# The first router of a mixture-of-experts block: eleven of 32 slot marks made by ScalarE, one group's logits computed between the next group's transposes, gather indices taken straight from the sums, and the passing of rows moved later

## The chip, the cores and the metric

The kernel runs on one core of a Trainium2 chip. The metric is the time of one execution on the device in microseconds (us), where lower is better. TensorE is called PE here, its weight loads PEld, VectorE DVE, ScalarE ACT, GpSimd POOL and SyncE SP, as in the rows of the profile.

## The reference, cut to what matters

4096 rows of 256 numbers go through three residual blocks: half a mixture-of-experts layer, a linear-attention layer with its own feed-forward part, and half a mixture-of-experts layer again. The change is in the first of them:

```
x = x + 0.5 * ffn(layernorm(x), w_switch, b_switch, w1, b1, w2, b2)

def ffn(x, ...):                       # x: 4096 rows, 8 experts, capacity 256
    probs  = softmax(x @ w_switch + b_switch)
    routes = probs.argmax(-1);  pmax = probs.max(-1)
    oh   = routes[:, None] == arange(8)
    pos  = (cumsum(oh, axis=0) * oh).sum(-1) - 1     # place in the expert's queue
    keep = pos < 256
    slot = where(keep, routes * 256 + pos, none)
    h = relu(rows_of_slots @ w1[e] + b1[e]);  y = h @ w2[e] + b2[e]
    out = where(keep, y[slot], x) * (pmax / stop_gradient(pmax))
```

A row that found no place keeps its own value. So each expert's first 256 rows are gathered, computed, and written back, and every row is also scaled and stored as if it had not been kept; the kept ones are overwritten.

## The kernel before, in words

**The work around the change.** The 4096 rows are 32 tiles of 128 rows (`NT`), in 8 groups of 4 tiles (`NG`, `GROUP`) and two batches of 16 tiles (`BATCH`). Every engine runs its own program, written out by hand in order; semaphores join them, and an instruction that waits holds all that stand behind it on its engine. Nothing is reordered by a scheduler.

**The pass over the rows.** SP loads the groups into `x_all`. PE transposes each tile (`turn_x`) into one of three PSUM banks, ACT copies it out (`turned_rows`); DVE takes mean and variance (`stats_a`). For each group PE then computes the logits (`logits_a`, which needs ACT's copies of that group and its copy of the logits before), ACT copies them out (`logits_out`), PE transposes them back (`turn_logits`). In each iteration PE does the four transposes of group g, then the logits of group g-1, then turns those of g-2.

**The router.** For each batch, DVE finds the best expert (`choose_a`, ten operations in the first batch, eight in the second), PE counts how many rows chose it earlier (`count_a`), and DVE makes from the count each row's place and one mark per tile: a 128x256 matrix in bf16 that is 1 where the place equals the column (`marks_a`). PE multiplies marks with row numbers (`number_slots_a`), which leaves in PSUM which row stands in each of the 2048 slots. DVE reduces these sums to `number_a`, makes of them the slot numbers and `token`, the indices of the gathers, and then the factors (`weigh_a`, `split_factors_a`).

**The experts.** GpSimd gathers the rows of an expert in two halves (`load_rows`), and gives 1/sqrt(variance) (`root_half`, `root_rows`); DVE normalises (`norm_rows`), PE transposes (`turn_rows`) and does two matrix products in units u of a quarter expert (`up`, and `down` two units later). For expert x, unit j, u is 4x+j. ACT does the first halves of the weights' high/low split (`high_weights`), DVE the second (`low_weights`). GpSimd sends finished rows with `send_rows(x)` at u = 4x+5; for expert 0 it first waits until all eight groups are stored (`s_astored`).

**Passing rows.** ACT scales the rows of a group in `x_all` (`pass_rows`), and SP stores the group in `mid_rows` (`store_quad`). Groups 0 to 3 are passed before the experts, 4 and 5 behind the first two copies of turned rows, 6 and 7 in units 0 to 3. SP also issues the experts' weight loads in the same queue: in step u of its loop it loads the weights of unit u+8, and the second load of such a pair waits until `down` of unit u is done.

## Time and profile before

| | |
|---|---|
| median of 3 runs | 696.75 us (694.77 to 698.53) |
| the profiled execution | 692.72 us, its span 691.0 us |
| PE busy | 648.0 us of the span |
| DVE, ACT, GpSimd busy | 517.4, 462.8 and 367.4 us |
| bytes moved by DMA | 95.61 MB, mean 138 GB/s |

The span is what the trace covers, and the execution's own time is 1.7 us more. A timeline row has start, length, engine, line, operation and tiles, and in brackets how long the engine stood idle before it and what ended that. Times in rows count from the start of the span; the length of "x4" is that of all four together. The expert phase of the first block begins at 44.37 us.

### The profile page before, as it was taken

The numbers are of one execution on the slowest core, as the hardware profiler recorded it, in microseconds if no ns is written. First come the engines' busy times: TensorE is split into PE (matmuls) and PEld (weight loads), VectorE is DVE, ScalarE is ACT, GpSimd is POOL, SyncE is SP. The second block draws the span as 40 slices with busy tenths as digits, with TensorE's granted clock in tenths as the row PEclk, the third lists the DMA queues.
The fourth block names the chain that finished last, engine by engine and source line by source line (L and its number), as shares of the span: only waits on it lengthen the run. The fifth ranks groups of instructions, "written<-read, shape, count | busy, mean of one in ns | idle before, by whom it ended". The sixth has DMA issues, their size and how long they took to land.

```text
span 691.0 us, 18005 instructions
## 1 busy us (share of the span) xinstructions
PE 648.0 (94%) x6398; PEld 570.5 (83%) x6398; DVE 517.4 (75%) x1371; ACT 462.8 (67%) x923; POOL 367.4 (53%) x542
## 2 busy tenths in 40 slices
PE   7789999997789999999999999999999994999997
PEld 5559998975679898988888888888988783899997
DVE  7968797624678877868778778888767558799982
ACT  6687777605467786767767667776763654798882
POOL 5254454634867545464673764845635653454422
PEclk9789999999999999999999999999999996999999
DMA  8499979424765555544565565564451534577750
GB/s 262 140 295 309 289 220 333 142 80 81 112 112 98 97 95 78 116 73 76 103 90 122 80 97 122 69 115 83 64 115 26 174 101 108 176 221 240 225 166 31
DMA packets 284803, 95.61 MB, mean 138 GB/s; under 512 B 213988, under 2 KB 281664, under 8 KB 284714
## 3 DMA queue, kind: packets, MB, share of 16 engines
q1 hardware_dynamic: 267610, 82.27, 49.4%
q0 software_dynamic: 4992, 11.47, 6.0%
q10 hardware_dynamic: 12112, 0.72, 1.1%
q8 instruction: 52, 0.85, 0.5%
q14 instruction: 37, 0.30, 0.1%
HBM read 65.09 MB, written 29.40 MB: 137 GB/s over the span
## 4 chain that ended last, share of the span: by engine, by line
PE 51%; DVE 8%; POOL 5%; issue 5%; ACT 3%; SPq 3%; DMA 1%; ACTq 1%; POOLq 0%; DVEq 0%
PE bank L1990 46%; PE bank L1999 5%; SPq L453 2%; POOL hids L920 2%; DMA qkv_rows<-feats 1%; SPq L459 1%; DVE den L1810 1%; DVE kv_ L1835 1%; DVE hn_ L1855 1%; DVE att_ L1808 1%; POOL sth L905 1%; ACTq L453 1%; POOL stz L889 1%; DVE ots L1801 0%; DVE feats L1930 0%
## 5 line engine op out<-in xcount | busy, mean ns | idle before, releaser
L1990 PE MATMUL bank<-hnts,up_w 128*128 128x512 f32 (+1 forms) x432 | 106.1, 382 | 0.1
L1990 PE MATMUL bank<-down_w,hids 128*128 128x256 f32 x768 | 104.5, 284 | 1.2 <-POOL hids L920 0.4
L920 POOL TENSOR_TENSOR hids<-hid,hids 128x512 fp32r<-128x512 f32 (+1 forms) x67 | 82.0, 1225 | 36.3 <-ACT hids L1212 36.2
L1990 PEld LDWEIGHTS bank<-down_w,hids 128*128 128x128 f32 x768 | 96.6, 189 | 4.2 <-POOL hids L920 1.8
L1990 PEld LDWEIGHTS bank<-hnts,up_w 128*128 128x128 f32 x432 | 71.3, 189 | 10.3 <-ACT hids L1212 0.3
L1990 PE MATMUL bank<-qkv_w,xnts 128*128 128x256 f32 (+1 forms) x384 | 76.9, 348 | 2.9 <-DVE xnts L1821 2.4
L1990 PEld LDWEIGHTS bank<-qkv_w,xnts 128*128 128x128 f32 x384 | 60.6, 189 | 20.0 <-issue 5.8
L1207 ACT ACTIVATE hid<-bank,cols 128x512 f32<-128x512 f32 (+1 forms) x72 | 45.7, 640 | 39.8 <-PE bank L1990 39.4
L886 POOL TENSOR_SCALAR stz<-stz 128x1 f32<-128x1 f32 x32 | 7.2, 226 | 115.2 <-DVE stz L1839 115.2
L1990 PE MATMUL bank<-xa_xt,a_w 128*128 128x256 f32 x384 | 52.6, 287 | 1.6 <-ACT xa_h L1048 1.1
L1990 PE MATMUL bank<-xb_xt,b_w 128*128 128x256 f32 x384 | 50.2, 280 | 0.7 <-DVE xb_xt L1502 0.5
L1990 PEld LDWEIGHTS bank<-xa_xt,a_w 128*128 128x128 f32 x384 | 47.9, 189 | 3.2 <-issue 1.5
L1990 PE MATMUL bank<-b_w2p,xb_hs 128*128 128x256 f32 x360 | 48.7, 285 | 0.0
L1990 PEld LDWEIGHTS bank<-xb_xt,b_w 128*128 128x128 f32 x384 | 47.4, 188 | 1.4 <-DVE xb_xt L1502 1.0
L1990 PEld LDWEIGHTS bank<-b_w2p,xb_hs 128*128 128x128 f32 x360 | 45.3, 191 | 0.0
L1212 ACT ACTIVATE hids<-bank,cols 128x512 fp32r<-128x512 f32 (+1 forms) x72 | 45.2, 635 | 0.0
L811 POOL DMA_INDIRECT mid_rows<-xa_fin,xa_slot x16 | 20.1, 1256 | 37.7 <-DVE xa_fin L1570 35.6
L811 POOL DMA_INDIRECT out_dram<-xb_fin,xb_slot x16 | 18.4, 1152 | 36.5 <-DVE xb_fin L1570 27.4
L1207 ACT ACT_TABLE_LOAD x29 | 37.2, 1283 | 0.5
L1855 DVE TENSOR_SCALAR hn_<-xo,sth 128x256 f32<-128x256 f32 x32 | 25.9, 808 | 15.5 <-POOL sth L905 15.1
L1048 ACT ACTIVATE xa_h<-bank,cols 128x256 f32<-128x256 f32 x64 | 26.7, 468 | 15.0 <-PE bank L1990 15.0
L1048 ACT ACTIVATE xb_h<-bank,cols 128x256 f32<-128x256 f32 x64 | 26.8, 470 | 14.8 <-PE bank L1990 14.8
(299 smaller groups left out, 1637.7 us busy)
## 6 DMA issues: line engine op xcount, KB each, us to landing
qkv_rows<-feats SPq DMA_DIRECT2D x32, 384.0 KB, 2.7
a_raw<-in_L_ffn_w_dram SPq DMA_DIRECT2D x32, 256.0 KB, 4.6
a_w<-in_L_ffn_w_dram SPq DMA_DIRECT2D x32, 256.0 KB, 4.7
b_raw<-in_L_ffn_w_dram SPq DMA_DIRECT2D x32, 256.0 KB, 3.4
b_w<-in_L_ffn_w_dram SPq DMA_DIRECT2D x32, 256.0 KB, 3.2
mid_rows<-x_all SPq DMA_DIRECT2D x8, 512.0 KB, 4.5
values<-qkv_rows SPq DMA_DIRECT2D x32, 128.0 KB, 3.0
late_rows<-x_ SPq DMA_DIRECT2D x8, 512.0 KB, 3.1
```

The source lines that it names most:

```text
L453: engine.dma_start(keys[i][t * HEADS:(t + 1) * HEADS, :, t * HD:(t + 1) * HD], qkv_rows[1, rows, :].rearrange("(s t) (h d) -> t h s d", t= ...
L459: engine.dma_start(queries[i][t * HD:(t + 1) * HD, :, t * HEADS:(t + 1) * HEADS], qkv_rows[0, rows, :].rearrange("(s t) (d h) -> t d s h", ...
L811: pool.indirect_dma_start(ex.target, bass.IndirectOffsetOnAxis(ap=ex.buf.slot[:, c - ex.first * ST], axis=0), ex.buf.fin[c % 4][:], None, ...
L886: pool.tensor_scalar(st[:, 8:9], st[:, 7:8], EPS, None, ALU.add).then_inc(s_rsz, 1)
L889: pool.tensor_tensor(st[:, 8:10], st[:, 8:10], minus_half[:, 0:2], ALU.pow).then_inc(s_rsz, 1)
L920: pool.tensor_tensor(hids[1][u % 3][:, 0:w], hid[u % 2][:, 0:w], f32(hids[0][u % 3][:, 0:w]), ALU.subtract).then_inc(s_hidl, 1)
L1048: act.activation(ex.buf.h[u % 4][:, i], dst[:, i * CAP:(i + 1) * CAP], ACT.Relu, bias=bias).then_inc(ex.sem.relu, 1)
L1207: act.activation(hid[u % 2][:, i * w:(i + 1) * w], bank[b][:, i * w:(i + 1) * w], ACT.Gelu, bias=cols[:, C_FCB + m:C_FCB + m + 1]).then_in ...
L1212: act.activation(hids[0][u % 3][:, i * w:(i + 1) * w], bank[b][:, i * w:(i + 1) * w], ACT.Gelu, bias=cols[:, C_FCB + m:C_FCB + m + 1]).the ...
L1855: dve.tensor_scalar(hn[:], xo[n % 3][:], st[:, 6:7], st[:, 8:9], ALU.subtract, ALU.mult).then_inc(s_hn, 1)
L1990: return pe.matmul(dst, left, right, start=start, stop=stop, skip_group_check=True)
L1999: return pe.matmul(dst, src, ident[:], is_transpose=True, start=start, stop=stop, skip_group_check=True)
```

## The change

Seven things are done:

- ACT makes 8 of the first batch's 16 marks and 3 of the second's, each with two operations instead of DVE's one: the absolute value of (place - column), and then relu(1 - that). DVE makes the other 21.
- PE computes the logits of group g-1 ahead of the last transpose of group g, and counts the first batch after its loop instead of ahead of the logits of group 6. ACT's conversion of the first expert's weights is cut in two, with the marks between.
- `token` is made from `number_a` in one operation (minus 1, at least 0), before the slot numbers instead of after them.
- PE does six products whose results nobody reads (`idle_products`), each of 512 columns, while it waits for the second batch.
- `weigh_a` is cut in two: the sum and its reciprocal are `top_a`, and the last two operations stand behind the second batch's marks.
- The first batch's marks by ACT are multiplied after the second count, ahead of the second batch's.
- Three groups instead of four are passed before the experts, one behind each half of the turned rows, and the last three in units 0 to 5. SP stores groups 0 to 4 ahead of its loop, and groups 5, 6 and 7 in steps u = 1, 3 and 5 of it, behind that step's weight loads.

```diff
@@ -473,6 +473,7 @@
         chunks = [(i, k, c) for i, (_, n, parts) in enumerate(pieces) for k in range(n)
                   for c in range(0, parts[-1][1] + parts[-1][2], D)]
         LATE = 10
+        PASSED_FIRST = 3
         LN_OF = {2: 2}
...
-            return 6 * b + 2
+            return 4 * b + 2
         def weighed(b):
-            return 11 * b + 6
+            return 9 * b + 8
+
+        def topped(b):
+
+            return 11 * b + 4
         def factored(b):
             return 9 * b + 13
+
+        MARKS_BY_ACT = (8, 3)
+
+        def marked_by_act(b):
+
+            return range((b + 1) * BATCH - MARKS_BY_ACT[b], (b + 1) * BATCH)
+
+        def marked_by_dve(b):
+
+            return range(b * BATCH, (b + 1) * BATCH - MARKS_BY_ACT[b])
+
+        def act_marks(b, half):
+
+            return NT + 2 * sum(MARKS_BY_ACT[:b]) + half * MARKS_BY_ACT[b]
         number_sums = bank[7][:, 0:E * ST * 2]
...
@@ -605,7 +624,7 @@
                     sp.wait_ge(xa.sem.rows[0][ST - 1], 16)
                     for c in range(PAIRS):
                         load_weights(1, xa, c)
-                if g < NG - 1:
+                if g < PASSED_FIRST + ST:
                     store_quad(g)
@@ -623,8 +642,8 @@
                 x, j = divmod(u, PAIRS)
                 if x + 2 < E:
                     load_weights(x + 2, xa, j)
-                if u == 0:
-                    store_quad(NG - 1)
+                if u % 2 == 1 and PASSED_FIRST + ST + u // 2 < NG:
+                    store_quad(PASSED_FIRST + ST + u // 2)
                 if u == LATE - 4:
                     sp.wait_ge(s_atab, 4)
...
@@ -1055,7 +1074,7 @@
                 for s in range(ST):
                     turn_half(s, ex)
                     if ex.first == 0:
-                        pass_rows(NG // 2 + s)
+                        pass_rows(PASSED_FIRST + s)
                 for u in range(ex.first * PAIRS, ex.end * PAIRS + 2):
                     x, j = divmod(u, PAIRS)
                     if x < ex.end:
@@ -1084,6 +1103,16 @@
                 these = slice(b * BATCH, (b + 1) * BATCH)
                 act.wait_ge(s_apick, 8 * b + 4)
                 act.activation(ex_a[:, these], sub_a[:, these], ACT.Exp).then_inc(s_aexp, 1)
+
+            def marks_a(b):
+                act.wait_ge(s_adisp, placed(b))
+                for n in marked_by_act(b):
+                    act.activation(mark_a[n][:], place[:], ACT.Abs, bias=small_a[:, 2, n:n + 1],
+                                   scale=-1.0).then_inc(s_axt, 1)
+                for i, n in enumerate(marked_by_act(b)):
+                    act.wait_ge(s_axt, act_marks(b, 0) + i + 1)
+                    act.activation(mark_a[n][:], mark_a[n][:], ACT.Relu, bias=first_wins[:, 0, E - 1:E],
+                                   scale=-1.0).then_inc(s_axt, 1)
             def pass_rows(g, part=range(GROUP)):
                 for n in range(g * GROUP + part.start, g * GROUP + part.stop):
...
@@ -1104,18 +1133,22 @@
                     logits_out(g - 1)
                 if g == NG - 1:
                     soften_a(0)
-            for c in range(PAIRS):
+            for c in range(PAIRS // 2):
+                high_weights(0, xa, c)
+            marks_a(0)
+            soften_a(1)
+            marks_a(1)
+            for c in range(PAIRS // 2, PAIRS):
                 high_weights(0, xa, c)
             act.wait_ge(s_mean, 2)
             act.copy(cols[:], bank[2][:, 0:col_rows]).then_inc(s_cols, 1)
-            soften_a(1)
-            for g in range(NG // 2):
+            for g in range(PASSED_FIRST):
                 pass_rows(g)
             def middle_weights(u):
-                if u < 2 * ST:
-                    pass_rows(NG // 2 + ST + u // 2, range(u % 2 * 2, u % 2 * 2 + 2))
+                if u < 2 * (NG - PASSED_FIRST - ST):
+                    pass_rows(PASSED_FIRST + ST + u // 2, range(u % 2 * 2, u % 2 * 2 + 2))
                 if LATE <= u < LATE + chunks_through(2):
                     i, k, c = chunks[u - LATE]
...
@@ -1571,13 +1604,22 @@
                                              scalar=ex.buf.scale[:, c - ex.first * ST], in1=buf[:, s], op0=ALU.mult,
                                              op1=ALU.add).then_inc(ex.sem.fin, 1)
+            def number_slots_a():
+
+                dve.tensor_scalar(empty_a[:], number_a[:], 0.0, float(NOWHERE + 1), ALU.is_equal, ALU.mult).then_inc(s_atab, 1)
+                dve.wait_ge(s_atab, 2)
+                dve.scalar_tensor_tensor(out=slot_a, in0=number_a[:], scalar=-1.0, in1=empty_a[:], op0=ALU.add,
+                                         op1=ALU.add).then_inc(s_atab, 1)
+
             def run_experts(ex, between=None, meanwhile=None):
                 if ex.slots is None:
-                    dve.wait_ge(s_atab, 3)
-                    dve.tensor_scalar(ex.buf.token[:], ex.buf.slot[:, :, 0], T - 1, None, ALU.min).then_inc(ex.sem.token, 1)
+                    dve.wait_ge(s_atab, 1)
+                    dve.tensor_scalar(ex.buf.token[:], number_a[:], -1.0, 0.0, ALU.add, ALU.max).then_inc(ex.sem.token, 1)
+                    number_slots_a()
                     dve.wait_ge(s_bias_raw, 16 * 7)
                     dve.tensor_copy(spread[:], ln_last[:].broadcast_to([1, P])).then_inc(s_foldq, 1)
                     split_factors_a(0)
+                    top_a(1)
                     weigh_a(1)
                     split_factors_a(1)
                 first_rows(ex, meanwhile)
...
@@ -1663,17 +1705,21 @@
                     dve.wait_ge(s_aseen, 2 * b + 2)
                     dve.tensor_tensor(seen_a[:, b + 1], recent_a[:, b], seen_a[:, b], ALU.add).then_inc(s_aseen, 1)
-            def weigh_a(b):
-                these, step = slice(b * BATCH, (b + 1) * BATCH), weighed(b) - 4
-                total, top, root = (small_a[:, i, these] for i in (3, 4, 0))
+            def top_a(b):
+                these, step = slice(b * BATCH, (b + 1) * BATCH), topped(b) - 2
+                total, top = (small_a[:, i, these] for i in (3, 4))
                 dve.wait_ge(s_aexp, b + 2)
                 dve.tensor_reduce(total, ex_a[:, these], AX, ALU.add).then_inc(s_adisp, 1)
                 dve.wait_ge(s_adisp, step + 1)
                 dve.reciprocal(top, total).then_inc(s_adisp, 1)
-                dve.wait_ge(s_adisp, step + 2)
+
+            def weigh_a(b):
+                these, step = slice(b * BATCH, (b + 1) * BATCH), weighed(b) - 2
+                top, root = (small_a[:, i, these] for i in (4, 0))
+                dve.wait_ge(s_adisp, topped(b))
                 dve.reciprocal(root, top).then_inc(s_adisp, 1)
-                dve.wait_ge(s_adisp, step + 3)
+                dve.wait_ge(s_adisp, step + 1)
                 dve.scalar_tensor_tensor(out=factor_a[:, these], in0=top, scalar=0.5, in1=root, op0=ALU.mult,
                                          op1=ALU.mult).then_inc(s_adisp, 1)
...
                 dve.wait_ge(s_adisp, step + 1)
                 dve.tensor_reduce(pos, cnt_a[:, these], AX, ALU.add).then_inc(s_adisp, 1)
                 dve.wait_ge(s_adisp, step + 2)
-                for n in range(b * BATCH, (b + 1) * BATCH):
+                for n in marked_by_dve(b):
                     dve.tensor_scalar(mark_a[n][:], place[:], small_a[:, 2, n:n + 1], None,
                                       ALU.is_equal).then_inc(s_amark, 1)
...
             marks_a(0)
             choose_a(1)
+            top_a(0)
+            marks_a(1)
             weigh_a(0)
-            marks_a(1)
             slot_a, scale_a = xa.buf.slot[:, :, 0], xa.buf.scale[:, :, 0]
             dve.wait_ge(s_aslot, NT)
             dve.tensor_reduce(number_a[:], number_sums.rearrange("p (c f) -> p c f", f=2), AX, ALU.add).then_inc(s_atab, 1)
-            dve.wait_ge(s_atab, 1)
-            dve.tensor_scalar(empty_a[:], number_a[:], 0.0, float(NOWHERE + 1), ALU.is_equal, ALU.mult).then_inc(s_atab, 1)
-            dve.wait_ge(s_atab, 2)
-            dve.scalar_tensor_tensor(out=slot_a, in0=number_a[:], scalar=-1.0, in1=empty_a[:], op0=ALU.add,
-                                     op1=ALU.add).then_inc(s_atab, 1)
             def middle_weights(u):
...
                     mm(dst[:, j + 1:], ones_bf[:], hot_a[:, b0 + j:b0 + j + 1].broadcast_to([P, BATCH - 1 - j, E]))
                 mm(dst, ones_bf[:], seen_a[:, b:b + 1].broadcast_to([P, BATCH, E]), stop=True).then_inc(s_acount, 1)
-            def number_slots_a(b):
+            def number_slots_a(b, rows):
                 sums = number_sums.rearrange("p (e s f) -> p s e f", s=ST, f=2)
                 pe.wait_ge(s_apick, 8 * (b + 1))
-                for n in range(b * BATCH, (b + 1) * BATCH):
-                    pe.wait_ge(s_amark, n + 1)
+                for n in rows:
+                    if n in marked_by_dve(b):
+                        pe.wait_ge(s_amark, n + 1 - sum(MARKS_BY_ACT[:b]))
+                    else:
+                        pe.wait_ge(s_axt, act_marks(b, 1) + n + 1 - rows.start)
                     for s in range(ST):
                         last = mm(sums[:, s], mark_a[n][:, s * P:(s + 1) * P], left_number_a[:, n], n == 0 and s == 0,
                                   n == NT - 1)
                     last.then_inc(s_aslot, 1)
             pe.wait_ge(s_pool_const, 6)
-            for g in range(NG + 2):
+            for g in range(NG + 1):
                 if g < NG:
                     for n in range(g * GROUP, (g + 1) * GROUP):
+                        if g >= 1 and n == (g + 1) * GROUP - 1:
+                            logits_a(g - 1)
...
@@ -2220,18 +2267,21 @@
                     for k in range(KD):
                         last = mm(bank[7][:, 0:E], mean_mat[:], switch_w[:, k], k == 0, k == KD - 1)
                     last.then_inc(s_mean, 1)
-                if g == NG - 1:
-                    count_a(0)
-                if 1 <= g <= NG:
+                if g == NG:
                     logits_a(g - 1)
-                if g >= 2:
+                if 2 <= g <= NG:
                     turn_logits(g - 2)
+            count_a(0)
+            turn_logits(NG - 1)
             pe.wait_ge(s_cols_src, 16 * 6)
             pe.matmul(bank[2][:, 0:col_rows], col_src[:], ident[0:col_rows, 0:col_rows], is_transpose=True,
                       start=True, stop=True).then_inc(s_mean, 1)
-            number_slots_a(0)
+            number_slots_a(0, marked_by_dve(0))
+            idle_products(6)
             count_a(1)
-            number_slots_a(1)
+            number_slots_a(0, marked_by_act(0))
+            number_slots_a(1, marked_by_dve(1))
+            number_slots_a(1, marked_by_act(1))
```

On ACT, between the logits of group 6 (`ra_lgt`) and the first passed rows (`x_all`), before:

```order
L1081 COPY ra_lgt<-bank 128x128 [waits a_logits_turned,a_logits]
L1016 CAST a_w<-a_raw 128x2x256 [waits experts_got10]
L1016 CAST a_w<-a_raw 128x2x256 [waits experts_got11]
L1016 CAST a_w<-a_raw 128x2x256 [waits experts_got12]
L1016 CAST a_w<-a_raw 128x2x256 [waits experts_got13]
L1110 COPY cols<-bank 128x80 [waits switch_mean_cols_turned_last_row_spread]
L1086 ACTIVATE ra_ex<-ra_sub 128x128 [waits a_picked]
L1092 ACTIVATE x_all<-x_all,ra_small 128x256 [waits a_pass_factors]
L1092 ACTIVATE x_all<-x_all,ra_small 128x256 x15
```

and now:

```order
L1100 COPY ra_lgt<-bank 128x128 [waits a_logits_turned,a_logits]
L1035 CAST a_w<-a_raw 128x2x256 [waits experts_got10]
L1035 CAST a_w<-a_raw 128x2x256 [waits experts_got11]
L1110 ACTIVATE ra_mark<-slot_place,ra_small 128x256 [waits a_dispatched]
L1110 ACTIVATE ra_mark<-slot_place,ra_small 128x256 x7
L1114 ACTIVATE ra_mark<-ra_mark,first_wins 128x256 [waits a_xt_made] x8
L1105 ACTIVATE ra_ex<-ra_sub 128x128 [waits a_picked]
L1110 ACTIVATE ra_mark<-slot_place,ra_small 128x256 [waits a_dispatched]
L1110 ACTIVATE ra_mark<-slot_place,ra_small 128x256 x2
L1114 ACTIVATE ra_mark<-ra_mark,first_wins 128x256 [waits a_xt_made] x3
L1035 CAST a_w<-a_raw 128x2x256 [waits experts_got12]
L1035 CAST a_w<-a_raw 128x2x256 [waits experts_got13]
```

Twenty-two operations on marks now stand between the two halves of the conversion `a_w<-a_raw`, with the second softmax (`ra_ex`) among them. Behind the rows shown come `cols` and the passing of twelve tiles instead of sixteen.

In SP's queue (`a_raw` and `a_w` are the two loads of a unit's weights, `mid_rows<-x_all` is the store of a group), before, from the stores of groups 4 to 6 to the loads of unit 10:

```order
L577 DMA mid_rows<-x_all 128x4x256 [waits a_passed] x3
L543 DMA a_raw<-in_L_ffn_w_dram 128x2x256 [waits experts_low1]
L555 DMA a_w<-in_L_ffn_w_dram 128x2x256 [waits experts_high1,experts_down]
L577 DMA mid_rows<-x_all 128x4x256 [waits a_passed]
L543 DMA a_raw<-in_L_ffn_w_dram 128x2x256 [waits experts_low1]
L555 DMA a_w<-in_L_ffn_w_dram 128x2x256 [waits experts_high1,experts_down]
L543 DMA a_raw<-in_L_ffn_w_dram 128x2x256 [waits experts_low1]
L555 DMA a_w<-in_L_ffn_w_dram 128x2x256 [waits experts_down]
```

and now, from the store of group 5 in step 1 of the loop to the store of group 7 in step 5:

```order
L596 DMA mid_rows<-x_all 128x4x256 [waits a_passed]
L562 DMA a_raw<-in_L_ffn_w_dram 128x2x256 [waits experts_low1]
L574 DMA a_w<-in_L_ffn_w_dram 128x2x256 [waits experts_down]
L562 DMA a_raw<-in_L_ffn_w_dram 128x2x256 [waits experts_low1]
L567 DMA b_row<-in_L_ffn_b_dram 128x256 [waits experts_biased]
L574 DMA a_w<-in_L_ffn_w_dram 128x2x256 [waits experts_down]
L596 DMA mid_rows<-x_all 128x4x256 [waits a_passed]
L562 DMA a_raw<-in_L_ffn_w_dram 128x2x256 [waits experts_low1]
L574 DMA a_w<-in_L_ffn_w_dram 128x2x256 [waits experts_high1,experts_down]
L562 DMA a_raw<-in_L_ffn_w_dram 128x2x256 [waits experts_low1]
L574 DMA a_w<-in_L_ffn_w_dram 128x2x256 [waits experts_high1,experts_down]
L596 DMA mid_rows<-x_all 128x4x256 [waits a_passed]
```

The store of group 7 stood behind the loads of unit 8 and now stands behind those of unit 13, with a wait for `down` (`experts_down`) in each pair between.

## Rows read from the trace of the kernel before

**Rows 1.** Two stretches: length; PE, PEld, DVE, ACT, POOL busy; clock; DMA; GB/s.
```profile
18.60:33.25 14.65, 11.09 (x161) 7.87 (x161) 13.58 (x60) 8.37 (x23) 2.31 (x6) 0.78 0.41 133
56.60:69.00 12.40, 12.40 (x95) 11.99 (x94) 10.06 (x22) 8.38 (x17) 4.58 (x6) 1.00 0.92 293
```

**Rows 2.** The timeline of VectorE in the router.
```profile
22.33 3.23 DVE L1712 TENSOR_SCALAR ra_mark<-slot_place,ra_small 128x256 bf16<-128x256 bf16 x16
25.47 0.29 DVE L1636 TENSOR_TENSOR ra_lg<-bank,ra_rstd 128x128 f32<-128x128 f32 x1
...
28.09 0.28 DVE L1671 TENSOR_REDUCE ra_small<-ra_ex 128x16 f32<-128x128 f32 x1
...
29.71 3.23 DVE L1712 TENSOR_SCALAR ra_mark<-slot_place,ra_small 128x256 bf16<-128x256 bf16 x16
33.25 0.19 DVE L1740 TENSOR_REDUCE ra_number<-bank 128x16 f32<-128x32 f32 x1 [0.32 <-PE bank L1990]
```

**Rows 3.** The timelines of VectorE, GpSimd and TensorE where the experts begin.
```profile
38.25 0.43 DVE L1490 BATCH_NORM_STATS2 xa_stat<-xa_rows 128x6 f32<-128x256 f32 x1
...
42.48 1.12 POOL L781 DMA_INDIRECT xa_rows<-in_L_attn_q_x_dram,xa_token  x1 [0.17 <-issue]
...
47.28 0.43 DVE L1526 BATCH_NORM_STATS2 xa_stat<-xa_rows 128x6 f32<-128x256 f32 x1 [1.91 <-DMA xa_rows<-in_L_attn_q_x_dram,xa_token]
...
49.89 0.33 PE L1999 MATMUL bank<-ident,xa_unit 128*128 128x128 f32 x1 [1.15 <-DVE xa_unit L1539]
```

**Rows 4.** The timeline of ScalarE in the first pass over the rows.
```profile
15.62 0.27 ACT L1081 COPY ra_lgt<-bank 128x128 f32<-128x128 f32 x1 [0.23 <-PE bank L1990]
16.07 1.33 ACT L1075 COPY xa_rows<-bank 128x256 f32<-128x256 f32 x4 [0.18 <-PE bank L1999]
```

**Rows 5.** The timeline of TensorE: the first count.
```profile
20.86 0.23 PE L1990 MATMUL bank<-ra_hot,upto 128*128 128x128 bf16 x1
```

**Rows 6.** ScalarE: three timeline rows, then groups by form (busy, mean ns).
```profile
23.56 2.18 ACT L1016 CAST a_w<-a_raw 128x512 fp32r<-128x512 f32 x4
...
30.47 7.97 ACT L1092 ACTIVATE x_all<-x_all,ra_small 128x256 f32<-128x256 f32 x16 [3.40 <-POOL ra_small L862]
...
46.06 0.84 ACT L1048 ACTIVATE xa_h<-bank,cols 128x256 f32<-128x256 f32 x2 [0.23 <-PE bank L1990]
...
L1137 ACT CAST down_w<-piece_raw 128x256 fp32r<-128x256 f32 x8 | 2.6, 405 | 0.0
...
L1098 ACT ACT_TABLE_LOAD x1 | 1.3, 1283 | 1.8 <-issue 1.8
```

**Rows 7.** The timeline of SyncE's DMA queue.
```profile
39.56 0.37 SPq L543 DMA_DIRECT2D a_raw<-in_L_ffn_w_dram  x1
...
56.61 0.37 SPq L577 DMA_DIRECT2D mid_rows<-x_all  x1
...
68.14 0.47 SPq L543 DMA_DIRECT2D a_raw<-in_L_ffn_w_dram  x1
```

**Rows 8.** The low part of expert 1's rows (VectorE), and unit 4 (TensorE).
```profile
53.11 0.69 DVE L1545 TENSOR_TENSOR xa_xt<-bank,xa_xt 128x512 fp32r<-128x512 f32 x1
...
55.02 1.77 PE L1990 MATMUL bank<-xa_xt,a_w 128*128 128x256 f32 x12
```

**Rows 9.** The timelines around the first sending of rows (GpSimd, VectorE, TensorE).
```profile
63.12 1.07 POOL L811 DMA_INDIRECT mid_rows<-xa_fin,xa_slot  x1 [6.03 <-DVE xa_fin L1570]
...
67.14 0.81 POOL L800 TENSOR_TENSOR xa_rstd<-xa_rstd,minus_half 128x2 f32<-128x2 f32 x1
...
68.31 0.73 DVE L1539 TENSOR_SCALAR xa_unit<-xa_rows,xa_mv,xa_rstd 128x256 f32<-128x256 f32 x2
...
75.17 0.60 PE L1999 MATMUL bank<-ident,xa_unit 128*128 128x128 f32 x4
```

**Rows 10.** The tile mid_rows up to 80 us: from issue to landing.
```profile
DMA to landing us min/median/max: 2.8/4.6/7.0
```

**Rows 11.** A stretch of the middle phase without work for TensorE, columns as in rows 1.
```profile
196.60:198.70 2.10, 0.00 (x0) 0.00 (x0) 1.11 (x3) 2.07 (x6) 0.38 (x1) 1.00 1.20 151
```

## The prediction

> **What bounds the kernel now.** The windows by stage show where PE stands idle. From 56.60 us on it has no gap at all, 12.40 of 12.40 us [rows 1], so a microsecond by which the experts start earlier is won, and one for which PE is held up there is lost. In the router, 18.60 to 33.25 us, PE is busy for 11.09 of 14.65 us and DVE for 13.58: DVE is the bound. I then read DVE's timeline. It has no gap: 16 marks from 22.33, the second choice from 25.47, the first factors from 28.09, the second place, 16 marks from 29.71 to 32.94, and the sums at 33.25, 0.31 behind the last mark [rows 2]. All that follows hangs on that last moment, which I call R: the first gathered rows are measured at R + 5.00, the fourth gather is issued at R + 9.23 and measured at R + 14.03, and for that PE waits 1.15 us at 49.89, R + 16.6 [rows 3].
>
> **The front, DVE.** A mark costs DVE (3.23 - 0.28)/15 = 0.20 us (0.28 for one alone, as for the reduction of like length at 28.09) [rows 2]. ACT's loop has 0.23 + 0.18 us of waits for PE in a period of 2.01 [rows 4]. With the logits ahead of the last transpose I let 0.25 of that go, in the last five groups 1.3 us. Group 7's logits then end at about 21.4, and the first count, which is moved behind them, starts at 21.45 instead of 20.86 [rows 5]. DVE's marks follow 1.47 behind it, as now: 22.92 instead of 22.33. Eight end at 24.5, the second choice takes 2.62 (25.47 to 28.09), to 27.1. From there to the second marks it is 1.62 now (28.09 to 29.71); two small operations of that move behind the marks, 0.5, so they start at 28.2. Thirteen end at 30.85, and with the two moved operations DVE is ready at 31.35. By DVE alone R would be 31.4.
>
> **The front, ACT.** The 22 operations for 11 marks are not in the trace. Bounds [rows 6]: relu from PSUM with one pointer operand, two in 0.84 at 0.47 each, is a step of 0.37; the passing of a tile in SBUF with two pointers, (7.97 - 0.59)/15 = 0.49. A cast of 256 columns in SBUF without a pointer is 0.405 long and the passing 0.59, so a pointer costs 0.09, and I take 0.49 - 0.09 = 0.40. ACT does two weight conversions first (0.52 each, from 2.18 for four) and is free at 22.9, when the place is there. 16 operations end at 29.3, the exponential at 29.6, the last six at 32.1. R = 32.1 + 0.31 = 32.4: ACT's last mark decides, and **0.85 us is won**; 1.85 at a step of 0.37 or less, where DVE decides, and at 0.49 R is 34.4 and 1.15 is lost.
>
> A mark thus costs 0.80 us on ACT and 0.20 on DVE. Eleven of them take 8.8 us of ACT, which stood idle for 3.40 ahead of the passing at 30.47 [rows 6], to save DVE 2.2. The Trainium skill, "ScalarE: Activation LUTs", section "Rules for kernel authors", says to use VectorE, not ScalarE, for relu, up to about three times faster in bf16. By that rule all marks would stay on DVE, and R would be 31.4 + 2.2 = 33.6, 0.3 worse than before; by the rows the sharing wins, because both engines work at once.
>
> One table load serves ACT's exponential, copies and relu up to here, at 1.28 us [rows 6]. If Abs needed another, four switches would lie in ACT's chain, 5.1 us. The same page of the Trainium skill, section "Table sets: the hidden batching unit" puts abs and relu into every set, so that none would come; no row here shows Abs.
>
> **Tokens and idle products: nothing.** The first gather starts 0.4 us earlier behind R, but DVE has the same operations ahead of its measuring at R + 5.00, which it reaches without a wait [rows 3]. The most it could bring is 0.4. The six idle products lie from 24.6 on, where PE waits for the second choice until about 26.7, and may take 2.1 us there free of charge.
>
> **Passing later: the ramp.** ACT is free at 32.1, converts two weights (1.1), copies `cols` (0.2) and passes 12 tiles (5.9), to 39.3 = R + 6.9; the first turned rows come at about R + 8. With 16 tiles it would be R + 8.9 and late by 0.9, so this edit saves what the marks would else cost. But group 3 is now passed behind the first turned rows, to R + 10.4, and its store stands ahead of expert 1's weights in SP's queue: their first load goes out at R + 10.8 instead of R + 6.3 (39.56) [rows 7]. ACT's conversion of it, its next rectification, and the copy of expert 1's rows come 1 to 2.3 us later. DVE's low part ends at 53.8 now and unit 4 starts at 55.02, 1.2 later [rows 8], so PE sees 0 to 1.1 of it. On the other side the fourth gather meets less traffic, and up to 0.6 of PE's wait of 1.15 may go. Bounds -0.6 and +1.1; I take **+0.4**.
>
> **Storing later: the large term.** Group 7's store goes out at 56.61 now. It moves behind the loads of unit 13, the second of which waits for `down` of unit 5. What stands next in that queue today is the load at 68.14, so that is the store's time [rows 7]. GpSimd's first sending, at 63.12 now [rows 9], waits for the stores, and 512 KB take 2.8 to 7.0 us to land, median 4.6 [rows 10]. It then starts at about 68.1 + 4.4 + 0.5 (a semaphore's way to GpSimd's DMA) = 73.0. Behind it on GpSimd stand a second indirect DMA and `root_rows(3)`. The sendings need 2.4 us, and with 0.3 and 1.25 for its two operations `root_rows(3)` ends 3.95 behind the start, at 77.0; it ends at 67.95 now. DVE waits for it at 68.31 with all its later work, normalises in 0.75, and lets PE's four transposes go at 77.85. They start at 75.17 now, without a gap [rows 9]: 2.7 lost, 2.9 with `down(8)`, which needs DVE's next operation too, and 3.2 with unit 12, whose low part is then 0.3 late. So **+3.2**; with a landing of 2.8 it is 1.6, with 6.5 it is 5.3. The rest of DVE's work is late by some 4 us, but has two units (6 us) of room. Since PE has no gap afterwards, nothing gives this back.
>
> **The sum.** -0.85 + 0.4 + 3.2 = +2.75. Against the profiled execution that is 692.72 + 2.75 = 695.5; the median of the runs shown is 4.0 above that execution, and 696.75 + 2.75 = **699.5**. A measurement of this kernel can tell about 0.5% (3.5 us) from no change.
>
> **The rivals.**
>
> (a) The clock falls while PE stands around 75.2 to 78. For: of 3.2 us only the four transposes are busy. Against: 2.1 us without any PE work from 196.60 left the clock at 1.00 [rows 11]. Were it half for 3.5 us, 1.75 would be added: 701.3.
>
> (b) The other side, faster: the late store holds nobody up. Then -0.85 + 0.4 = -0.45 is left, or with the quicker ACT and the relieved gather -1.85 - 0.6 = -2.45: 694.3 to 696.3. It decides if the sending starts before 75.17 - 4.85 = 70.3, so if the store is issued before 65.4 or the waits are not in the order that I read. Against: 10 us of delay at the sending exceed the 7 between 68.31 and 75.17.
>
> (c) Far faster: the late store holds nobody up, the gather's whole 1.15 goes and R is 31.0, by a shorter loop of the transposes too: -2.25 - 1.15 = -3.4, 693.3. Nothing in DVE's gapless chain speaks for it.
>
> (d) ACT's marks are dearer: at 0.49 a step R is 34.4 and the whole +1.15 + 0.4 + 3.2 = 4.75, 701.5; with two table loads besides 704.0. The Trainium skill's rule for relu (the same page, "Rules for kernel authors") points this way: the marks that it would leave on DVE are what decides R then.
>
> **How the numbers follow.** My forecast, the stall at the full clock, 0.56; (a) 0.17; (b) 0.15; (c) 0.03; (d) 0.09. The forecast's own spread is 697.3 to 701.6, by the landing, the step and the ramp, and some 0.15 of its 0.56 lies above 700.25. With most of (a) and (d) slower gets 0.36; (c) and the quick end of (b) give faster 0.07; the same is left with 0.57. The range leaves out (c), the quick end of (b) and the far end of (d): 695.5 to 703.0.
>
> **What would show it.** In the new profile: ACT's marks at a step of 0.40 and the last near 32.1; the reduction to `number_a` at 32.4; the store of group 7 near 67.7 (all being 0.45 earlier); GpSimd idle for some 15 us ahead of its first sending at 72.5 in place of 6.03; DVE waiting 8 us for `root_rows(3)`; PE idle for 2.5 us ahead of the transposes of unit 10. If PE has no such gap, the largest term is wrong; if the last mark ends well off 32, the front is.

## The result, and the profile after

The changed kernel takes 702.11 us (median of 4 runs, 701.49 to 704.58), the kernel before 695.76 in the runs beside it (4 runs, 693.0 to 698.53). The ratio is 1.0102, with a 95% interval of 1.0071 to 1.0134: some 7 us slower (4.9 to 9.3), where 2.75 were forecast. The time lies in the range of 695.5 to 703.0, but it is clearly slower, to which the prediction gave 0.36, and not within the 3.5 us of no change, to which it gave 0.57.

The profiled execution took 704.58 us, span 702.8, which is the slowest of its runs, and the profiled one of before (692.72) lies below its median, so the two traces differ by 11.8 us. Up to the first product behind the experts it is 6.57 us (152.28 against 145.71). The other 5.2 come later, where nothing was changed: from there to the end the changed kernel took 550.5 us and the kernel before 545.3, but with the same code there the profiles of the twelve experiments took anything from 544.5 to 550.2. So only the first 150 us are read for the change.

**The front.** DVE in the router of the changed kernel; the rows answer to [rows 2]:

```profile
19.29 0.29 DVE L1678 TENSOR_TENSOR ra_lg<-bank,ra_rstd 128x128 f32<-128x128 f32 x1 [0.74 <-PE bank L2041]
25.87 1.66 DVE L1758 TENSOR_SCALAR ra_mark<-slot_place,ra_small 128x256 bf16<-128x256 bf16 x8
27.45 0.28 DVE L1678 TENSOR_TENSOR ra_lg<-bank,ra_rstd 128x128 f32<-128x128 f32 x1
31.20 2.64 DVE L1758 TENSOR_SCALAR ra_mark<-slot_place,ra_small 128x256 bf16<-128x256 bf16 x13
35.27 0.19 DVE L1787 TENSOR_REDUCE ra_number<-bank 128x16 f32<-128x32 f32 x1 [1.05 <-PE bank L2032]
```

R, the reduction to `number_a`, is at 35.27, not at 32.4: 2.02 us later than in [rows 2], where 0.85 earlier was forecast. DVE's first marks start at 25.87 (forecast 22.9), and at the end DVE, whose chain had no gap before, waits 1.05 us for PE, which waits for ACT's last mark. ACT in the same stretch:

```profile
24.37 0.27 ACT L1100 COPY ra_lgt<-bank 128x128 f32<-128x128 f32 x1 [0.64 <-PE bank L2032]
24.54 1.14 ACT L1035 CAST a_w<-a_raw 128x512 fp32r<-128x512 f32 x2
25.87 3.30 ACT L1110 ACTIVATE ra_mark<-slot_place,ra_small 128x256 bf16<-128x256 bf16 x8 [0.20 <-DVE ra_small L1755]
29.08 3.28 ACT L1114 ACTIVATE ra_mark<-ra_mark,first_wins 128x256 bf16<-128x256 bf16 x8
32.27 0.29 ACT L1105 ACTIVATE ra_ex<-ra_sub 128x128 f32<-128x128 f32 x1
...
33.66 1.29 ACT L1114 ACTIVATE ra_mark<-ra_mark,first_wins 128x256 bf16<-128x256 bf16 x3
```

From 25.87 to 34.95 ACT works without a gap. The step is (33.66 + 1.29 - 25.87 - 0.29)/22 = 0.40 us, as estimated, and the chain of 9.1 us has the length forecast (9.2, from 22.9 to 32.1). It began 3.0 us too late. ACT was done with its two conversions at 25.68, and the last thing that it waited for, 0.20 us, was the place, which DVE makes from the first count. What preceded both on PE, last logits and first count, answers to [rows 5]:

```profile
23.67 0.65 PE L2032 MATMUL bank<-xa_rows,centred 128*32 128x128 f32 x16 [0.61 <-ACT ra_lgt L1100]
24.25 0.33 PE L2041 MATMUL bank<-ident,ra_lgt 128*128 128x128 f32 x1
24.41 0.22 PE L2032 MATMUL bank<-ra_hot,upto 128*128 128x128 bf16 x1
```

and in the kernel before the last logits were copied 0.98 us earlier:

```profile
23.39 0.27 ACT L1081 COPY ra_lgt<-bank 128x128 f32<-128x128 f32 x1 [0.64 <-PE bank L1990]
```

When that copy starts differs from execution to execution even where the code up to there is the same: from 22.59 to 24.37 over six kernels with the new loop, from 23.39 to 24.17 over eight with the old one. From the copy to R, however, it is 10.89 to 10.91 us in all six, and 9.86 in the kernel before (9.84 in experiment 3, whose front is the same). So of the 2.02 us only 1.04 belong to the new order behind the copy; the other 0.98 is within what one execution differs from another.

**The stall.** Timelines of PE, DVE, GpSimd and SP's queue in the changed kernel, which answer to [rows 3, 7, 8, 9]:

```profile
46.43 4.37 PE L2032 MATMUL bank<-xa_xt,a_w 128*128 128x256 f32 x36 [0.49 <-DVE xa_xt L1535]
53.86 1.65 PE L2032 MATMUL bank<-xa_xt,a_w 128*128 128x256 f32 x12 [0.90 <-ACT xa_h L1067]
57.71 1.65 PE L2032 MATMUL bank<-xa_xt,a_w 128*128 128x256 f32 x12 [0.47 <-DVE xa_xt L1578]
65.45 0.60 PE L2041 MATMUL bank<-ident,xa_unit 128*128 128x128 f32 x4
...
81.41 0.92 PE L2041 MATMUL bank<-ident,xa_unit 128*128 128x128 f32 x4 [3.51 <-DVE xa_unit L1572]
82.10 2.90 PE L2032 MATMUL bank<-a_w2p,xa_hs 128*128 128x256 f32 x12
...
95.39 0.60 PE L2041 MATMUL bank<-ident,xa_unit 128*128 128x128 f32 x4
...
80.62 0.73 DVE L1572 TENSOR_SCALAR xa_unit<-xa_rows,xa_mv,xa_rstd 128x256 f32<-128x256 f32 x2 [8.37 <-POOL xa_rstd L819]
...
77.15 1.07 POOL L830 DMA_INDIRECT mid_rows<-xa_fin,xa_slot  x1 [16.63 <-DMA mid_rows<-x_all]
...
70.71 0.47 SPq L596 DMA_DIRECT2D mid_rows<-x_all  x1
```

Read from below it is the chain that the prediction described: the store at 70.71, the sending 6.44 us later after 16.63 us of waiting, DVE idle for 8.37 us until `root_rows(3)`, PE idle for 3.51 us. PE's clock did not survive that. Windows of the changed kernel, columns as in [rows 1]:

```profile
80.00:81.00 1.00, 0.00 (x0) 0.00 (x0) 0.38 (x2) 0.00 (x0) 0.81 (x2) 1.00 1.09 382
81.00:82.00 1.00, 0.59 (x4) 0.52 (x4) 1.00 (x4) 0.00 (x0) 0.97 (x1) 0.83 1.10 395
82.00:84.00 2.00, 2.00 (x11) 1.93 (x10) 2.00 (x5) 1.10 (x2) 1.71 (x1) 0.50 0.53 156
84.00:86.00 2.00, 2.00 (x15) 2.00 (x14) 2.00 (x4) 0.00 (x0) 1.64 (x1) 0.73 0.54 179
86.00:88.00 2.00, 2.00 (x20) 2.00 (x19) 2.00 (x6) 1.83 (x4) 1.70 (x2) 1.00 0.94 281
```

The granted clock is at 0.50, so 1.2 instead of 2.4 GHz, from 82 to about 85 us. From these transposes to the next expert's it is 95.39 - 81.41 = 13.98 us, where 12.29 is the rule (87.46 - 75.17 in the kernel before): 1.69 us for the clock. The windows agree: at 0.50 for 2 us and at 0.73 for another 2 a time of 1.54 is lost, and 0.1 ahead of them.

**Where the 6.57 us arose**, by the same transposes in both traces. PE in the kernel before, beside the 75.17 of [rows 9]:

```profile
62.89 0.60 PE L1999 MATMUL bank<-ident,xa_unit 128*128 128x128 f32 x4
...
87.46 0.60 PE L1999 MATMUL bank<-ident,xa_unit 128*128 128x128 f32 x4
...
108.78 1.62 PE L1990 MATMUL bank<-xa_xt,a_w 128*128 128x256 f32 x12 [1.12 <-ACT xa_h L1048]
```

The front gave 2.02. From R to the transposes of expert 2 it is 30.18 us (65.45 - 35.27) against 29.64: ramp 0.54. At those of expert 3 the distance is 6.24 (81.41 against 75.17), so the stall took 3.68; at the next it is 7.93, so the clock took 1.69. Later 1.36 came back: the kernel before loses that much in expert 5, where its PE waits 1.12 us for ACT at 108.78, and ACT for the 1 MB load of `fc_w`. The changed kernel, 8 us later, does not meet this wait. Nor do some of the experiments, and others meet a larger one, so these microseconds say nothing of the change.

### The profile page after: what moved, and what is told of

The parts are those of the page before. It is cut to its first block, busy times and chain, and to the rows that moved or that the text cites. A ratio compares the mean times of both kernels' runs of the same rounds, so it can differ in the third digit from the quotient of the medians.

```text
span 702.8 us, 18030 instructions
## 1 busy us (share of the span) xinstructions
PE 655.1 (93%) x6404; PEld 574.8 (82%) x6404; DVE 517.8 (74%) x1360; ACT 470.3 (67%) x945; POOL 369.7 (53%) x542
## 4 chain that ended last, share of the span: by engine, by line
PE 65%; DVE 8%; issue 6%; ACT 6%; POOL 5%; DMA 4%; SPq 4%; ACTq 1%; POOLq 0%; DVEq 0%
PE bank L2032 58%; PE bank L2041 7%; SPq L453 2%; POOL hids L939 2%; SPq L459 1%; DMA mid_rows<-x_all 1%; DMA a_w<-in_L_ffn_w_dram 1%; DVE den L1852 1%; DMA x_all<-in_L_attn_q_x_dram 1%; ACT ra_mark L1110 1%; DMA qkv_rows<-feats 1%; ACT ra_mark L1114 1%; DVE kv_ L1877 1%; DMA keys<-qkv_rows 1%; DVE att_ L1850 1%
## 5 line engine op out<-in xcount | busy, mean ns | idle before, releaser
L2032 PEld LDWEIGHTS bank<-hnts,up_w 128*128 128x128 f32 x432 | 71.2, 189 | 10.4 <-ACT hids L1245 0.3
L830 POOL DMA_INDIRECT mid_rows<-xa_fin,xa_slot x16 | 22.1, 1380 | 39.9 <-DVE xa_fin L1603 20.6
L1217 ACT COPY kvt_<-bank 128x512 f32<-128x512 f32 x32 | 18.8, 587 | 28.9 <-PE bank L2032 28.9
L2032 PE MATMUL bank<-keys,values 128*32 128x128 f32 x1024 | 34.3, 273 | 3.9 <-DMA keys<-qkv_rows 3.1
```

What stands on the lines that cost most here:

```text
L830: pool.indirect_dma_start(ex.target, bass.IndirectOffsetOnAxis(ap=ex.buf.slot[:, c - ex.first * ST], axis=0), ex.buf.fin[c % 4][:], None, ...
L1217: act.copy(kvt[:], bank[B_KV][:].rearrange("p (i c) -> p i c", i=4)).then_inc(s_kvt, 1)
L2032: return pe.matmul(dst, left, right, start=start, stop=stop, skip_group_check=True)
```

## The experiments

"Before" is measured anew with each group of kernels; its median was 694.6 to 695.8. In the table R and T2 (the start of the transposes of expert 2) are from each kernel's profile, and the stall is PE's idle time ahead of expert 3's transposes. Each R and T2 is of one execution.

| kernel | median (runs) | ratio to before, 95% | R | T2 - R | stall |
|---|---|---|---|---|---|
| before | 695.76 (4) | | 33.25 | 29.64 | 0 |
| changed | 702.11 (4) | 1.0102 (1.0071 to 1.0134) | 35.27 | 30.18 | 3.51 |
| 1 passing undone | 697.86 (12) | 1.0034 (1.0016 to 1.0053) | 35.03 | 29.69 | 0 |
| 2 loop undone | 703.72 (6) | 1.0131 (1.0105 to 1.0158) | 34.61 | 30.03 | 4.37 |
| 3 passing alone | 704.87 (6) | 1.0117 (1.0084 to 1.0150) | 34.01 | 33.09 | 3.74 |
| 4 roots ahead | 701.05 (6) | 1.0076 (1.0053 to 1.0098) | 34.33 | 31.27 | 0 |
| 5 store earlier | 697.73 (6) | 1.0043 (1.0025 to 1.0060) | 35.07 | 31.22 | 0 |
| 6 marks by DVE | 696.69 (11) | 1.0024 (1.0009 to 1.0039) | 33.49 | 31.34 | 0 |
| 7 eight marks | 694.24 (11) | 1.0000 (0.9981 to 1.0018) | 31.79 | 29.72 | 0 |
| 8 gather ahead too | 696.36 (9) | 1.0024 (1.0003 to 1.0045) | 33.48 | 31.85 | 0 |
| 9 combined | 695.01 (12) | 1.0005 (0.9984 to 1.0025) | 31.49 | 31.71 | 0 |
| 10 without idle products | 694.70 (12) | 0.9999 (0.9975 to 1.0022) | 32.28 | 30.96 | 0 |
| 11 loads first | 705.01 (6) | 1.0130 (1.0098 to 1.0162) | 34.33 | 32.61 | 3.71 |
| 12 loads behind | 696.30 (12) | 1.0016 (0.9996 to 1.0037) | 32.01 | 33.06 | 0 |

**1. The passing undone.** The changed kernel, but:

```diff
-                if g < PASSED_FIRST + ST:
+                if g < NG - 1:
                     store_quad(g)
-                if u % 2 == 1 and PASSED_FIRST + ST + u // 2 < NG:
-                    store_quad(PASSED_FIRST + ST + u // 2)
+                if u == 0:
+                    store_quad(NG - 1)
```

and `NG // 2` for `PASSED_FIRST` where rows are passed.

> The changed kernel with the passing and the stores as before: four groups passed before the experts, group 7 passed in units 2 and 3, its store behind unit 8's loads. Everything else stays. Theory 1 (the late store holds GpSimd, GpSimd's root_rows(3) holds DVE and so PE, and the clock falls in the stall: 5.4 us; ramp 0.7 us): no idle time of PE ahead of the transposes of unit 10 and no clock below 1.00 from 57 us on, so 5.4 less; the gather relief of 1.27 us is lost again, but expert 1's weights come earlier; ACT has sixteen tiles to pass and is 0.9 to 2 us late for the first turned rows. Net 4 to 6 us less than the changed kernel, and 1 to 3 us more than the kernel before, which is the front. Theory 2 (the front is the main loss, and the stall only takes up slack that is given back later): 0 to 2 us less than the changed kernel. Theory 3 (the eleven marks on ACT are the loss, since ACT now becomes late for everything): ACT late for the first turned rows by 2 us or more and the time stays 4 us or more above the kernel before.

The stall is gone and about 4.7 us with it (1.0102 against 1.0034). Both are within what the first theory said. R is 1.78 us later than in the kernel before, and so are expert 3's transposes (77.00 against 75.17), although ACT passes sixteen tiles and unit 0 begins at R + 11.75 instead of R + 11.12. But the remaining 2.4 us over the kernel before (1.1 to 3.7) can't be put down to the front alone. PE further on in this kernel:

```profile
101.58 0.60 PE L2041 MATMUL bank<-ident,xa_unit 128*128 128x128 f32 x4
...
112.02 2.90 PE L2032 MATMUL bank<-xa_xt,a_w 128*128 128x256 f32 x12 [2.52 <-ACT xa_h L1067]
```

ACT waits 7.02 us for the load of `fc_w`, PE 2.52 us for ACT, and the clock falls to 0.50. The next transposes are at 118.12, 16.54 us later instead of 12.29: 4.25 us lost, where the kernel before loses 1.36 at the same place.

**2. The loop undone.** TensorE's loop as before:

```diff
-                        if g >= 1 and n == (g + 1) * GROUP - 1:
-                            logits_a(g - 1)
                         turn_x(n)
...
+                if g == NG - 1:
+                    count_a(0)
+                if 1 <= g <= NG:
+                    logits_a(g - 1)
```

> The changed kernel with TensorE's loop as before: a group's logits behind all four transposes of the next group, the first count ahead of the logits of group 6. Everything else stays. Theory 1 (the first count comes 3.5 us later because it now stands behind the loop, and this and nothing else made the front late): the count at about 21 us instead of 24.4, the reduction to number_a at 32 to 33 instead of 35.27, and so 2 to 3 us less in all, with the later stall unchanged at about 5 us. Rival (the loop was late because of loads and a cold TensorE at the begin, whatever the order in it): the reduction stays above 34.5 and the whole time within 1 us of the changed kernel.

The first count is at 21.48, near the 21 expected, and R gains only 0.66, 0.31 of it behind the last copy of logits (10.59 us instead of 10.90). Timelines of ACT, DVE and GpSimd in this kernel:

```profile
24.02 0.27 ACT L1100 COPY ra_lgt<-bank 128x128 f32<-128x128 f32 x1 [0.64 <-PE bank L2032]
24.18 1.14 ACT L1035 CAST a_w<-a_raw 128x512 fp32r<-128x512 f32 x2
25.22 3.30 ACT L1110 ACTIVATE ra_mark<-slot_place,ra_small 128x256 bf16<-128x256 bf16 x8
...
28.47 2.64 DVE L1758 TENSOR_SCALAR ra_mark<-slot_place,ra_small 128x256 bf16<-128x256 bf16 x13
34.61 0.19 DVE L1787 TENSOR_REDUCE ra_number<-bank 128x16 f32<-128x32 f32 x1 [3.13 <-PE bank L2032]
...
77.18 1.07 POOL L830 DMA_INDIRECT mid_rows<-xa_fin,xa_slot  x1 [17.50 <-DMA mid_rows<-x_all]
```

My expectation was wrong: R stays above 34.5, as the rival said, and no time is won (1.0131 against 1.0102, whose intervals overlap). DVE is now ready 3.1 us early and waits for ACT's marks, since ACT itself is kept until 25.2 by the last logits. In the changed kernel the place came 0.2 us behind ACT's conversions, so undoing the one alone leaves the other. What bounds the router here is when ACT starts and how many marks it has, not the place of the count. The 0.66 us did not reach the end either: the first sending starts at 77.18, as in the changed kernel, because the store, 0.8 us earlier, took 0.85 longer to it. The clock was at 0.50 from 80 to 86, and the next transposes came 14.79 us later instead of 13.98.

**3. The passing alone**, applied to the kernel before (the first experiment's edit the other way round).

> The kernel before with the later passing and the later stores alone (three groups before the experts, group 7's store in step 5 of SyncE's loop). Theory 1: the front as in the kernel before (the reduction at 33.2), ramp within 1 us of it, and the stall ahead of the transposes of unit 10 with its fallen clock whole: 5 to 6 us more than the kernel before. Theory 2 (the stall arises only because the changed front shifts the phases): 0 to 2 us more.

It costs 8.1 us (5.8 to 10.4), where 5 to 6 were expected. The stall is whole (3.74 us, then the half clock), though the front is that of before. The surprise is the ramp: T2 - R is 33.09. ACT waits 3.29 us at 51.48 for expert 1's weights, loaded at 45.33, PE 2.43 us for ACT at 54.62, and there the clock falls too (12 products of that kind in 2.61 us instead of 1.65).

**4. Roots ahead.** The store stays late, and GpSimd does `root_rows(3)` before `send_rows(0)`.

```diff
+                            if px == 0:
+                                root_rows(px + 3, ex)
                             send_rows(px, ex)
-                            if px + 3 < ex.end:
+                            if px > 0 and px + 3 < ex.end:
                                 root_rows(px + 3, ex)
```

> The changed kernel with GpSimd's root_rows(3) ahead of send_rows(0) instead of behind it; the store of group 7 stays as late as it is. Theory 1 (the late store costs only through what is queued behind the sending on GpSimd): the sending is as late as before (about 77 us), but root_rows(3) ends near 68, DVE and PE have no gap at unit 10, the clock stays at 1.00, and 4.5 to 5.5 us are won against the changed kernel. Rival (the store's own traffic, or the late sending, collides with the weight loads or with the later gathers): 0 to 2 us won, and PE waits elsewhere between 75 and 90 us.

PE and GpSimd in this kernel:

```profile
77.88 0.60 PE L2043 MATMUL bank<-ident,xa_unit 128*128 128x128 f32 x4
...
90.37 1.61 PE L2034 MATMUL bank<-xa_xt,a_w 128*128 128x256 f32 x12 [1.42 <-ACT xa_h L1069]
...
77.96 1.25 POOL L830 DMA_INDIRECT mid_rows<-xa_fin,xa_slot  x1 [5.62 <-DMA mid_rows<-x_all]
...
80.81 1.01 POOL L800 DMA_INDIRECT xa_rows<-in_L_attn_q_x_dram,xa_token  x1 [0.30 <-issue]
```

The stall at expert 3 is gone, as the theory says, but only some 1.8 us are won by the two ratios, whose intervals overlap; that is the rival's outcome, with PE waiting elsewhere. The gather of expert 4's rows is queued behind the sending too: it goes out at 80.81 instead of 68.15, DVE waits 4.24 us for it at 86.66, and PE 1.42 us at 90.37 and 0.97 at 98.50. The transposes of experts 4 and 5 come 14.01 and 14.39 us behind those before them, instead of 12.29, so these waits and shorter ones cost 3.8 us. I had looked only at the first victim in GpSimd's queue.

**5. The store one unit earlier**, the changed kernel with

```diff
-                if u % 2 == 1 and PASSED_FIRST + ST + u // 2 < NG:
+                if u in (1, 3, 4):
```

> The changed kernel with the store of group 7 one step earlier in SyncE's loop (behind unit 12's loads instead of unit 13's); nothing else moves. Theory 1 (GpSimd's order behind the store decides, one for one with the time of the store): the store goes out near 67.7 instead of 70.71, the first sending near 74.1 instead of 77.15, root_rows(3) ends near 77.4, PE waits 0.5 to 1 us instead of 3.51 ahead of the transposes of unit 10, the clock stays at 1.00, and 4 to 5 us are won in all against the changed kernel. Rival (traffic decides: the store then lands later, since it meets the loads of units 13 to 15): the sending stays within 1 us of 77 and less than 1.5 us are won.

The store goes out at 68.71 and the sending at 74.23. PE has no wait at expert 3 and the clock stays up; 4.1 us are won by the two ratios, as expected. So the loss has an edge: with one unit less delay, 2.8 us against PE's own time (the store is 2.42 behind expert 2's transposes instead of 5.26), the stall of 3.51 and the clock's 1.69 both vanish. Not all is gone: from expert 3's transposes to expert 4's it is 13.05 us, 0.76 above the rule.

**8. The gather ahead too.** As experiment 4, with `load_rows(4)` also ahead of the first sending.

> The changed kernel with GpSimd's root_rows(3) and the gather of expert 4's rows both ahead of the first sending; the store stays late. Theory 1 (what the late store still cost with only root_rows(3) ahead, some 4 us, was the gather queued behind the sending: it went out at 80.8 instead of 68.2): the gather at about 72, no wait of TensorE between 75 and 105 us, and 5 to 7 us less than the changed kernel, 695 to 697. Rival (the bunched traffic between 77 and 88 us, with DMA at 1.0 to 1.1, is the cause): TensorE still waits 2 us or more between 85 and 105 us, and less than 3 us are won.

The gather is at 71.35, the sending as late as ever (77.03), and PE has no wait between 75 and 105 us. Some 5.4 us are won, as expected, and as much as the stall and the clock took in the profile of the changed kernel (3.68 + 1.69). The bunched traffic is not the cause.

**6. All marks by DVE**, `MARKS_BY_ACT = (0, 0)`, with passing and loop as before; and **7. eight marks**, `(5, 3)`, with ACT's four weight conversions behind them:

```diff
-        MARKS_BY_ACT = (8, 3)
+        MARKS_BY_ACT = (5, 3)
...
-            for c in range(PAIRS // 2):
-                high_weights(0, xa, c)
             marks_a(0)
             soften_a(1)
             marks_a(1)
-            for c in range(PAIRS // 2, PAIRS):
+            for c in range(PAIRS):
                 high_weights(0, xa, c)
```

> The changed kernel with passing and stores and TensorE's loop as before, and all 32 marks by VectorE, none by ScalarE. What stays of the change: the direct tokens, the idle products, the two later operations of the factors, the cut conversion. Theory 1 (ScalarE's marks are the bound of the changed router, because ScalarE is free only at 25.2): the reduction at 33.0 to 33.7 and 1 to 2 us less than the first experiment (the one with the passing undone), so 695 to 697, within 0.2% of the kernel before. Rival (sharing the marks does help, the loss of the front being the loop's alone): the reduction at 34.5 or later.

> As the kernel with all marks by VectorE, but with five and three marks by ScalarE (8 instead of 11), and ScalarE's conversion of four weights wholly behind the marks. By the steps measured (0.40 us an operation on ScalarE from 24.2 on, 0.20 us a mark on VectorE from 22.95 on) ScalarE's last mark ends at 31.0 and VectorE's at 31.7, and the reduction is at 32.0: 1.3 us ahead of the kernel before and 2.6 ahead of the kernel with all eleven. Theory 1: 1 to 1.5 us less than the kernel with all marks by VectorE, 694.5 to 696, and faster than the kernel before by 0 to 1 us. Rival (the later conversion of weights and ScalarE's later passing eat it): the reduction at 32.0 and yet the first product of unit 0 not earlier than in the kernel before.

Timelines of DVE, ACT and PE with eight marks:

```profile
28.66 2.64 DVE L1756 TENSOR_SCALAR ra_mark<-slot_place,ra_small 128x256 bf16<-128x256 bf16 x13
31.79 0.19 DVE L1785 TENSOR_REDUCE ra_number<-bank 128x16 f32<-128x32 f32 x1
...
29.88 1.29 ACT L1114 ACTIVATE ra_mark<-ra_mark,first_wins 128x256 bf16<-128x256 bf16 x3
...
41.13 0.35 ACT L1047 CAST xa_xt<-bank 128x256 fp32r<-128x256 f32 x1
...
42.92 0.44 PE L2039 MATMUL bank<-ident,xa_unit 128*128 128x128 f32 x2 [1.97 <-DVE xa_unit L1527]
```

With the same loop R is 33.49 with none on ACT, 34.61 with eleven (experiment 2) and 31.79 with eight, where 32.0 was worked out from the steps: ACT ends at 31.17, DVE at 31.30. Counted from the last copy of logits it is 9.37, 10.59 and 7.97 us, so the order doesn't hang on when the loop ended.

In time less is shown. Experiment 6 is only 0.7 us below experiment 1 by the ratios, with overlapping intervals, and 0.24% above the kernel before, so its theory held for R alone. R is 0.24 us later there than before, and yet T2 - R is 31.34 instead of 29.64. ACT in experiment 6, to be read beside [rows 6]:

```profile
34.77 7.97 ACT L1121 ACTIVATE x_all<-x_all,ra_small 128x256 f32<-128x256 f32 x16 [3.56 <-POOL ra_small L881]
```

ACT is idle, but begins to pass 4.30 us later than the 30.47 of before, because `weigh_a` now stands behind the second batch's marks and GpSimd makes the factors of the passing from it. GpSimd's four operations also hold the first gather, to R + 1.43 instead of R + 1.12, and unit 0 begins at R + 12.39 instead of R + 11.12. This is a price of moving those two operations that the prediction didn't have; it counted only the 0.5 us that they free. In the changed kernel it is hidden, since ACT itself is busy until 36.0. No run undoes that part alone.

Experiment 7 takes 1.7 us less than 6 by the ratios, and 2.4 less than experiment 1; it also differs from 6 in where the conversions stand. It only equals the kernel before (0.9981 to 1.0018). R is 1.46 us earlier than there, but unit 0 begins at R + 12.49 instead of R + 11.12, at 44.28 against 44.37, because ACT passes sixteen tiles up to 41.1 and DVE and PE wait for its copy. That is what the rival said: R near 32.0 and unit 0 hardly earlier. It is the same lateness that made the change pass fewer groups. But the profile doesn't end level: PE has no wait at expert 1 here, and expert 2's transposes are at 61.51 against 62.89. Why the medians show nothing of this 1.4 us stays open; the interval is 1.3 us wide on either side.

**9. Combined**, an attempt to have both: experiment 7's router with three groups passed first, expert 1's loads ahead of the store of group 3 (`if g == PASSED_FIRST:`), and group 7's store in step 3. **10** is the same without `idle_products(6)` in the router, **12** with the loads behind that store again, and **11** is the changed kernel with the loads ahead.

> The parts that paid, together: TensorE's loop as before, five and three marks by ScalarE with the weight conversion behind them, three groups passed ahead of the experts (so that ScalarE is free for the first turned rows, for which it was 2.2 us late with four), expert 1's weights in SyncE's queue ahead of the store of group 3, and group 7's store in step 3 of its loop. Theory 1: the reduction at 31.8; unit 0 begins at about 43 instead of 44.28 (five and three marks with four groups), no wait of TensorE at units 4 and 10; 1 to 1.5 us less than that kernel, 692.5 to 693.5, 0.2 to 0.4% faster than the kernel before. Rival (expert 1's loads now meet the first gathers, and the fourth gather meets the stores of groups 3 and 4): unit 0 not before 44, or a wait of TensorE at the transposes of expert 1, and no gain over 694.2.

> The combined kernel without the six idle products in the router. Theory 1 (they are free only where TensorE's clock is up; in the two profiles in which it was down they took 2.7 us and the second count came 0.5 to 0.9 us late behind them): the second count never late, the reduction at 31.8 or up to 0.5 us earlier on average, the whole time within 0.5 us of the combined kernel and rather below it. Rival (they keep the clock up for what follows): the clock falls before the marks' products, the reduction is 0.3 us later or more, and so is the end.

> The changed kernel with expert 1's weights in SyncE's queue ahead of the store of group 3; nothing else. Theory 1 (the ramp's loss of 0.7 us, and ScalarE's waits of 1.26 and 0.55 us for the weights, come from the loads standing behind that store): these waits gone, TensorE's waits of 0.90 and 0.47 us at units 2 and 4 gone; the units up to 9 run 0.7 to 1.4 us earlier, and since the store of group 7 waits for one of them, the stall at unit 10 moves with them: 0.7 to 1.5 us less than the changed kernel. Rival (the wait for the fourth gather, relieved in the changed kernel, returns): TensorE waits 0.5 to 1.2 us for the transposes of expert 1, and nothing is won.

> The combined kernel with expert 1's weights in SyncE's queue behind the store of group 3 again, as in the changed kernel. Theory 1 (a tug of war for the DMA engines between expert 1's loads and the fourth gather, in which the loads' place only decides who waits): no wait of TensorE at the transposes of expert 1 (1.75 us in the combined kernel), but ScalarE waits for the weights again and TensorE for it at units 2 and 4, 0.9 to 1.4 us in all; the whole time within 1 us of the combined kernel and of the kernel with four groups ahead, 694 to 695.5. Rival (the loads behind are better, and with ScalarE free in time both are had): unit 0 at R + 11.1, waits at units 2 and 4 below 0.5 us in all, and 692.5 to 693.5.

No gain over the kernel before in 9, 10 and 12, and 11 is no better than the changed kernel (1.0130 against 1.0102, with overlapping intervals). PE in experiment 11:

```profile
52.27 0.66 PE L2041 MATMUL bank<-ident,xa_unit 128*128 128x128 f32 x4 [2.54 <-DVE xa_unit L1572]
```

and ACT and PE in experiment 12:

```profile
49.52 0.62 ACT L1037 CAST a_w<-a_raw 128x512 fp32r<-128x512 f32 x1 [3.24 <-DMA a_raw<-in_L_ffn_w_dram]
...
47.96 0.60 PE L2041 MATMUL bank<-ident,xa_unit 128*128 128x128 f32 x4
52.68 2.90 PE L2032 MATMUL bank<-xa_xt,a_w 128*128 128x256 f32 x12 [2.39 <-ACT xa_h L1069]
```

With the loads ahead, the fourth gather comes late: DVE waits for it 3.30 us in 11 and 2.52 in 9, and PE 2.54 and 1.75 at expert 1's transposes. With the loads behind, in 12, the gather is nearly in time (0.28) and the weights are late; PE waits 2.39 us at unit 2 and loses clock as well. So the rivals of 9 and 11 came out, that of 11 with a wait of 2.54 where it said 0.5 to 1.2, and the first theory of 12 in its mechanism, with a price above its bound (2.4 against 0.9 to 1.4, and 696.3 against at most 695.5).

The place in the queue doesn't decide alone. In experiments 4 and 5, with the loads behind, both came late: DVE waited 2.13 and 1.64 us for the gather and ACT 2.40 and 2.28 for the weights. In experiment 7, with four groups first, PE had neither wait; in experiment 6, with the same queue, it waited 1.52 us for the gather, and before 1.15 [rows 3]. What tips this balance stays open.

The idle products, priced at nothing, do something. In 9 the second count's 15 products took 0.65 us and the second marks began 3.76 behind the second choice; without them, in 10, PE idled 1.93 us ahead of the count, the clock was at 0.52 from 27 to 30 us, the 15 took 1.03, and it was 4.20. In experiment 4, whose clock was down already (0.64 from 24 to 29), they took 2.72 us themselves and the distance was 4.68. So the router part of 10's rival came true, but the medians of 9 and 10 can't be told apart.

## Why the prediction was right and wrong

**The stall, +3.2: right in mechanism, too small.** Queue, order on GpSimd, DVE's wait and PE's gap were as described, and experiments 1 and 5 take the stall away at the store, 4 and 8 on GpSimd. Front and ramp moved PE by 2.56 us and the store by 2.57, from 68.14 to 70.71. The term that was sized too small is the way from store to sending: 6.44 us instead of 4.9. The landing took 5.6 of it, where the sum had 4.4 (the median of [rows 10] is 4.6), and the sending began 0.8 behind it, where the sum had 0.5, a figure that no row shows. From the sending to PE's transposes it was 4.26 instead of 4.85, so the transposes came 3.68 us late against 2.7 forecast, 3.51 of it without work. The 0.5 for what follows at full clock can't be told from the clock's loss. Rival (a), the fallen clock, is true besides: 1.69 where it said 1.75. It had 0.17, argued down by [rows 11], 2.1 us of idleness through which the clock stayed up; but the gap forecast was 2.7 us, and that row says nothing of a longer one.

**The front, -0.85: wrong, +2.02.** The step that failed is "ACT ... is free at 22.9". With it goes "group 7's logits then end at about 21.4", from which it was counted: they ended at 24.3, and the first count was at 24.41 instead of 21.45. [Rows 6] has ACT's conversions at 23.56, behind the copy of the last logits. Two of them end at 24.65, and 9.2 of marks and 0.31 more give R = 34.2 even without any change of the loop. The logits ended at 23.3 before, so 21.4 is 1.9 earlier; the shortened loop explains 1.3 of that, and the rest has no row. Against it the last two sets of logits lie 1.73 us apart in the changed kernel and 1.12 in the one before, because the second waits for ACT's copies. The loop gained nothing that can be seen: its period fell from 2.01 to 1.90 (1.76 forecast), but group 1's transposes began at 7.34 instead of 6.53 behind a load, and a second set of logits took 1.08 us instead of 0.65. Over the kernels with the new loop R varies from 33.48 to 35.27, and all but 0.02 of that arises ahead of the last copy of logits. From that copy on the new order takes 10.90 us against 9.86, so it could win only if the copy came 1.04 us earlier, and the rest of the 2.02 is luck of the execution. The step of 0.40 was right.

**ScalarE against VectorE.** By the Trainium skill, "ScalarE: Activation LUTs", section "Rules for kernel authors", relu belongs on VectorE. Against eleven marks on ScalarE this was the better advice (R 33.49, where the prediction had 33.6 by that rule, against 34.61), against eight with the conversions behind them it was not (31.79). With what the same page's "Table sets: the hidden batching unit" says of abs and relu, that every set has them, the trace agrees: they followed each other at 0.40 us with no load of a table between.

**The ramp, +0.4: direction right, size low.** The profiled pair shows 0.54. Over the table, T2 - R is 29.64 to 31.34 in the four kernels with four groups ahead (mean 30.1) and 30.03 to 33.09 in the ten with three (mean 31.6; three of these also order the loads otherwise). So it may be more like 1.5, but five kernels with the same passing and the same queue up to there (the changed one, 2, 4, 5 and 8) lie anywhere from 30.03 to 31.85, and one profile of each can't size it. The half that I had weighed, gather relieved and weights late, is there in both directions; what I missed is that PE's wait for the weights can reach 2.4 us and take the clock.

**Tokens and rival (b).** The token came 0.22 behind R instead of 0.65, and unit 0 no earlier for it (R + 11.16). Rivals (b) and (c) did not come true; (d) named ACT's marks for the late R, but for the wrong reason: they were not dearer, but late.

**By kind of loss**, by the ratios: the passing 4.7 us on top of the changed front, give or take 2.5, and everything else 2.4, give or take 1.3. How the 2.4 divide among the marks, the loop, the moved factors and the wait for `fc_w` isn't shown. Experiment 3 gives the passing 8.1 alone, which the intervals only just allow; why its ramp was worse is open. That the time fell inside the range owes something to luck: front, ramp and stall were all forecast too low, the fallen clock came on top, and the range reached up to 703.0 only because of the dearer marks of rival (d), which did not come true.

## What to carry to other kernels

When work is moved to an idle engine, start its chain from the row in which that engine is last kept and the row that makes its input, whichever is later, and not from a time worked out without them: at the price foreseen, eleven marks put R 1.1 us later than none, and eight marks with the conversions behind them 1.7 earlier. When two operations are moved off a chain, look for who else waits for their result: here the passing, 4.3 us. When a transfer is issued later, list everything behind its waiter on that queue, not only the first: here the root, then the gather, each enough to stall TensorE. And such a delay costs nothing up to a point and then its excess plus the clock: one unit less removed the stall and the fallen clock, so move the waiter, or the store by one step, before giving up the idea.

## What the runs showed that I had not expected

- How often a wait of TensorE costs clock besides. After the idle 3.51 us it was at 1.2 GHz until about 85 us. After idle times of 2.39 and 2.43 us in experiments 12 and 3, 12 products took 2.90 and 2.61 us instead of 1.65; after one of 2.14 in experiment 8 they took 1.82, with the clock at 0.53 from 54 to 56 us; after one of 2.10 in experiment 11 (at 119.55) 1.65.
- In the first 13 us the logits' 16 products took 1.08 us instead of 0.65, once in the kernel before and twice in the changed one, although the granted clock of those stretches reads 1.00. No run here explains it.
- Expert 1's weights and the fourth gather are seldom both in time. The gather was waited for 2.5 and 3.3 us in experiments 9 and 11, with the loads ahead (1.9 before), the weights 1.3 to 3.3 us with three groups passed first and the loads behind, and in experiments 4 and 5 both.
- How exact a hand-ordered stretch is: the same order from the last copy of logits to R took 10.89 to 10.91 us in six kernels, while the moment of that copy differed by 1.8 us. A difference between two profiles is best read from the last point at which they agree.
